# Splitting projected queries and keys into three bf16 parts: residuals by TensorE matmuls, or by VectorE subtractions in PSUM

## The reference, cut to what matters

```python
xn = _layernorm(x)
q, k, v = split(xn @ w_attn, 3)                 # 16 heads of 8 channels
scores = q @ k.T / sqrt(8) + causal + logw      # logw: a decay per head over the distance
att = softmax(scores); y = att @ v
out = x + y @ w_proj + moe(xn)                  # softmax router, top 2 of 8, silu, 128 -> 512 -> 128
```

## Time and profile before

| | |
|---|---|
| time, median of 3 runs | 726.49 us (723.21 to 731.6) |
| the profiled execution | 724.6 us, of which the span from first to last instruction is 722.8 us |
| PE busy | 580.9 us (80%) |
| POOL busy | 413.9 us (57%) |
| DVE busy | 340.2 us (47%) |
| ACT busy | 291.3 us (40%) |

### The profile page before, as it was taken

One profiled execution on the slowest core, in us unless ns is written; L12 is line 12 of the kernel. 1 busy time (PEld: TensorE's weight loads), 2 busy tenths in 40 slices (PEclk: granted clock), 3 DMA queues, 4 the chain that ended last, 5 costly groups with the idle time before them and its releaser, 6 DMA issues.

```text
span 722.8 us, 13966 instructions
## 1 busy us (share of the span) xinstructions
PE 580.9 (80%) x4558; PEld 396.4 (55%) x4572; DVE 340.2 (47%) x1396; ACT 291.3 (40%) x521; POOL 413.9 (57%) x674
## 2 busy tenths in 40 slices
PE   0696200999999999999999999999859998899840
PEld 0275000565555555565555555665558988898840
DVE  6504800466566565475565655677213222222225
ACT  7121000565555555555555555556512222222210
POOL 1300478777686677686786776789224444344432
PEclk9999999999999999999999999999969999999985
DMA  8952011222240331322312312310715565555538
GB/s 208 181 161 88 26 52 41 67 66 71 74 125 25 124 93 50 102 71 77 101 48 75 115 34 74 104 56 16 220 41 167 171 186 173 168 178 176 174 124 274
DMA packets 76564, 79.05 MB, mean 109 GB/s; under 512 B 8766, under 2 KB 59712, under 8 KB 76496
## 3 DMA queue, kind: packets, MB, share of 16 engines
q1 hardware_dynamic: 72144, 69.70, 34.4%
q0 software_dynamic: 4352, 8.47, 3.4%
HBM read 46.49 MB, written 30.02 MB: 106 GB/s over the span
## 4 chain that ended last, share of the span: by engine, by line
PE 71%; DVE 11%; POOL 5%; issue 5%; DMA 4%; SPq 2%; ACT 1%; POOLq 0%; DVEq 0%
PE psT L1014 18%; PE psO L1026 11%; PE ps L1104 11%; PE psT L1114 9%; PE psM L967 8%; PE ps L993 6%; DVE scores L881 5%; POOL rows_dram L592 4%; PE psO L957 2%; PE psM L976 1%; DMA x_all<-x 1%; PE psM L1095 1%; PE psM L969 1%; DVE x_all L428 1%; PE ps L1059 1%
## 5 line engine op out<-in xcount | busy, mean ns | idle before, releaser
L610 POOL TENSOR_SCALAR scores<-scores,row_max 128x256 f32<-128x256 f32 (+3 forms) x512 | 264.0, 533 | 92.0 <-DVE row_max L881 89.8
L881 DVE CUSTOM_DVE_ANT_0 scores<-ps,wdist 128x256 f32<-128x256 f32 (+3 forms) x512 | 222.2, 487 | 175.3 <-PE ps L993 175.2
L676 ACT ACTIVATE probs<-psT 128x512 f32<-128x512 f32 x320 | 173.9, 595 | 137.1 <-PE psT L1014 137.1
L1014 PE MATMUL psT<-ident,scores 128*128 128x128 f32 x1280 | 175.2, 281 | 36.5 <-POOL scores L610 36.5
L1014 PEld LDWEIGHTS psT<-ident,scores 128*128 128x128 f32 x1280 | 140.5, 142 | 74.3 <-POOL scores L610 47.7
L626 POOL DMA_INDIRECT picked_dram<-values,row_ring x72 | 70.7, 982 | 98.1 <-DVE values L924 93.0
L1026 PE MATMUL psO<-probs,values 128*32 128x512 f32 (+3 forms) x1024 | 94.8, 444 | 0.0
L712 ACT ACTIVATE probs<-ps 128x512 f32<-128x512 f32 x72 | 43.0, 597 | 126.6 <-PE ps L1104 126.6
L1104 PE MATMUL ps<-values,wdist 128*128 128x128 f32 x576 | 81.0, 285 | 12.4 <-issue 11.6
L1104 PEld LDWEIGHTS ps<-values,wdist 128*128 128x128 f32 x576 | 71.4, 196 | 18.9 <-issue 18.2
L1114 PE MATMUL psT<-wdist,probs 128*128 x576 | 77.3, 278 | 0.0
(11 more groups left out here) (119 smaller groups left out, 367.9 us busy)
## 6 DMA issues: line engine op xcount, KB each, us to landing
wdist<-w1t SPq DMA_DIRECT2D x72, 256.0 KB, 3.2
k_rows<-k_dram SPq DMA_DIRECT2D x64, 96.0 KB, 2.5
q_rows<-q_dram SPq DMA_DIRECT2D x64, 96.0 KB, 2.4
rows_dram<-probs SPq DMA_DIRECT2D x1, 4680.0 KB, 34.8
row_ring<-rows_dram SPq DMA_DIRECT2D x72, 65.0 KB, 2.5
probs<-picked_dram SPq DMA_DIRECT2D x8, 512.0 KB, 7.5
k_dram<-k_parts SPq DMA_DIRECT2D x8, 384.0 KB, 2.4
q_dram<-q_parts SPq DMA_DIRECT2D x8, 384.0 KB
```

The lines of the kernel that those rows point to most:

```text
L610: last = nc.gpsimd.tensor_scalar(part, part, -1.0, row_max[:, r, tile, quad:quad + 1], ALU.mult, ALU.add)
L676: nc.scalar.activation(probs[:, at.ring(2), w, :], psT[:, w % 2], ACT.Exp, scale=-1.0).then_inc(exp_ready, 1)
L881: last = nc.vector.tensor_tensor_reduce(out=scores[:, r, u, col:col + n], in0=bank[:, col:col + n], in1=wdist[:, at.g * QUADS + quad, SEQ ...
L1014: last = nc.tensor.transpose(psT[:, w % 2, place * P:(place + 1) * P], scores[:, at.ring(2), u, col + key * P:col + (key + 1) * P], ident[:])
```

## The change

The projection is made once per batch for keys and once for queries (KA, QA). Its hi part is rounded by ACT as before. The residual is no longer made anew by TensorE: DVE subtracts hi from `psM` in place (KR, QR, `rest_step`), ACT rounds what is left to mid (KM, QM, `mid_step`), and DVE subtracts mid from it and writes the result, rounded to bf16, as lo (KL, QL, `lo_step`). The steps KB, KC, QB, QC and the tile `minus_ident` go. `psM` stays taken from KA to KL. KR stands behind P1(1) in the slot, KM behind TE 2-4, KL behind TE 4-6 and PV 2 and ahead of P1(3). Three semaphores are new (`hi_ready`, `rest_ready`, `mid_ready`). In the start DVE runs the prologue's four subtractions after it has normalised batch 2.

```diff
+    per_batch("KR", -3)
+    per_batch("QR", -2)
     step("TE", n - 1, NGROUP, 2, 4)
     step("PV", n - 2, NGROUP, 1)
-    per_batch("KB", -3)
-    per_batch("QB", -2)
+    per_batch("KM", -3)
+    per_batch("QM", -2)
     per_batch("PJ", 8)
     step("P1", n, NGROUP, 2)
     step("TE", n - 1, NGROUP, 4, 6)
     step("PV", n - 2, NGROUP, 2)
+    per_batch("KL", -3)
+    per_batch("QL", -2)
     step("P1", n, NGROUP, 3)
     step("TE", n - 1, NGROUP, 6, 8)
     step("PV", n - 2, NGROUP, 3)
-    per_batch("KC", -3)
     per_batch("KW", -3)
-    per_batch("QC", -2)
     per_batch("QW", -2)
...
-PROLOGUE = [("KA", 0), ("KB", 0), ("KC", 0), ("KW", 0), ("QA", 0), ("QB", 0), ("QC", 0), ("QW", 0), ("V", 0),
+PROLOGUE = [("KA", 0), ("KR", 0), ("KM", 0), ("KL", 0), ("KW", 0), ("QA", 0), ("QR", 0), ("QM", 0), ("QL", 0), ("QW", 0),
+            ("V", 0),
             ("KD", 0), ("QD", 0)]
-MISC_KINDS = ("KA", "KB", "KC", "QA", "QB", "QC", "V", "NT", "YT", "PJ")
+MISC_KINDS = ("KA", "QA", "V", "NT", "YT", "PJ")
...
                 def keys_write(at):
-                    sp.wait_ge(misc_free, at.misc("KC", 1))
+                    sp.wait_ge(misc_free, at.misc("KA", 1))
...
+                def hi_step(kind, parts, written):
                     def step(at):
                         act.wait_ge(misc_full, at.misc(kind, 1))
-                        if number == 0 and at.c > 0:
+                        if at.c > 0:
                             act.wait_ge(written, at.batches(48))
-                        nc.scalar.activation(parts[:, number], psM[:], ACT.Copy).then_inc(misc_free, 1)
+                        nc.scalar.activation(parts[:, 0], psM[:], ACT.Copy).then_inc(hi_ready, 1)
+                def mid_step(number, parts):
+                    def step(at):
+                        act.wait_ge(rest_ready, at.batches(2, number))
+                        nc.scalar.activation(parts[:, 1], psM[:], ACT.Copy).then_inc(mid_ready, 1)
...
+                def rest_step(number, parts):
+                    def step(at):
+                        dve.wait_ge(hi_ready, at.batches(2, number))
+                        nc.vector.tensor_tensor(psM[:], psM[:], parts[:, 0], ALU.subtract).then_inc(rest_ready, 1)
+                def lo_step(number, parts):
+                    def step(at):
+                        dve.wait_ge(mid_ready, at.batches(2, number))
+                        nc.vector.tensor_tensor(parts[:, 2], psM[:], parts[:, 1], ALU.subtract).then_inc(misc_free, 1)
...
                 for b in range(1, BATCH):
                     normalise(b)
+                    if b == 2:
+                        run_prologue(number_parts)
...
                     def step(at):
                         misc_use(at, kind)
                         if kind == "KA" and (at.c >= 2 * GROUPS):
                             pe.wait_ge(xt_loaded, at.batches(16, -16))
-                        last = mm(psM[:], w, xt[:, at.parity, :], start=True, stop=not parts)
-                        for part in parts:
-                            last = mm(psM[:], minus_ident[:], part, start=False, stop=part is parts[-1])
-                        last.then_inc(misc_full, 1)
+                        mm(psM[:], w, xt[:, at.parity, :], start=True, stop=True).then_inc(misc_full, 1)
```

More of the change, by code:

```diff
@@ L121, in per_batch @@
             b = (n - phase) // GROUPS
-            if 0 <= b < BATCH and b >= {"XT": 2, "KA": 1, "KB": 1, "KC": 1, "KW": 1, "QA": 1, "QB": 1, "QC": 1, "QW": 1,
-                                          "V": 1}.get(kind, 0):
+            if 0 <= b < BATCH and b >= {"XT": 2, "V": 1}.get(kind, 0 if kind in ("YT", "PJ") else 1):
                 steps.append((kind, b * GROUPS - n))
@@ L259, in build @@
         ident = sb("ident", [P, P])
-        minus_ident = sb("minus_ident", [P, P], BF16)
         minus_half = sb("minus_half", [P, NTILE])
@@ L364, in build @@
         misc_free = sem("misc_free")
+        hi_ready = sem("hi_ready")
+        rest_ready = sem("rest_ready")
+        mid_ready = sem("mid_ready")
         k_written = sem("k_written")
@@ L654, in _ @@
                         last.then_inc(wdist_ready, 1)
-                def part_step(kind, parts, number, written):
+                def hi_step(kind, parts, written):
                     def step(at):
                         act.wait_ge(misc_full, at.misc(kind, 1))
-                        if number == 0 and at.c > 0:
+                        if at.c > 0:
                             act.wait_ge(written, at.batches(48))
-                        nc.scalar.activation(parts[:, number], psM[:], ACT.Copy).then_inc(misc_free, 1)
+                        nc.scalar.activation(parts[:, 0], psM[:], ACT.Copy).then_inc(hi_ready, 1)
+                    return step
+                def mid_step(number, parts):
+                    def step(at):
+                        act.wait_ge(rest_ready, at.batches(2, number))
+                        nc.scalar.activation(parts[:, 1], psM[:], ACT.Copy).then_inc(mid_ready, 1)
                     return step
@@ L766, in normalise @@
                     last.then_inc(xn_ready, 1)
+                def rest_step(number, parts):
+                    def step(at):
+                        dve.wait_ge(hi_ready, at.batches(2, number))
+                        nc.vector.tensor_tensor(psM[:], psM[:], parts[:, 0], ALU.subtract).then_inc(rest_ready, 1)
+                    return step
+                def lo_step(number, parts):
+                    def step(at):
+                        dve.wait_ge(mid_ready, at.batches(2, number))
+                        nc.vector.tensor_tensor(parts[:, 2], psM[:], parts[:, 1], ALU.subtract).then_inc(misc_free, 1)
+                    return step
+                number_parts = {"KR": rest_step(1, k_parts), "KL": lo_step(1, k_parts),
+                                "QR": rest_step(2, q_parts), "QL": lo_step(2, q_parts)}
                 dve.wait_ge(rstd_ready, 1)
@@ L959, in start_logits, with all_heads_step @@
                     return last
-                def all_heads_step(kind, w, parts):
+                def all_heads_step(kind, w):
                     def step(at):
@@ L1045, in pj_step @@
                     last.then_inc(misc_full, 1)
-                k_less, q_less = ([parts[:, 0], parts[:, 1]] for parts in (k_parts, q_parts))
-                w_k = w_qkv[:, C:2 * C]
-                parts = {"QA": all_heads_step("QA", w_q[:], []), "QB": all_heads_step("QB", w_q[:], q_less[:1]),
-                         "QC": all_heads_step("QC", w_q[:], q_less), "KA": all_heads_step("KA", w_k, []),
-                         "KB": all_heads_step("KB", w_k, k_less[:1]), "KC": all_heads_step("KC", w_k, k_less),
+                parts = {"QA": all_heads_step("QA", w_q[:]), "KA": all_heads_step("KA", w_qkv[:, C:2 * C]),
                          "V": v_step, "P1": p1_step, "TE": turn_step,
```

12 lines of the change are left out of this document (5 added, 7 removed).

## The result

The changed kernel takes 682.34 us (median of 4 executions, 674.33 to 683.83) against 726.19 us in the same comparison (median of 4, 723.21 to 731.6): 43.9 us less, ratio 0.9366 with a 95% interval of 0.9274 to 0.9457. Forecast were 679 us and 46.4 us less. The profiled execution took 682.88 us, its span 681.1.

The account below looks back on a forecast made before the run. PE was taken to bound the attention, with the prologue also on the path: 38.8 us from the slots plus 7.6 from the start, 46.4 in all, took the profiled 724.6 us to 678.2, forecast as a 679 us median, range 672 to 690.

Parts of the forecast that it names:

- PE is the bound: Attention: PE, busy 96% or more in K, Q and V slots, sets the pace; DVE and POOL keep up.
- 2.77 us a slot, 38.8 in all: Attention: dropping KB (1.28 us) and KC (1.49), likewise for queries, saves 2.77 us in each of 14 K and Q slots.
- The additions cost nothing at 0.69 us: K and Q slots: two added DVE subtractions of 0.69 us each fit without delaying PE.
- the two bounds: Price of one DVE subtraction: 0.4 us at the least, 1.4 us at the most, around the chosen 0.69.
- The margin: K and Q slots: DVE can run about 0.4 us late, ahead of P1(4), before PE is delayed.
- The late-DVE rival: K and Q slots: subtractions of 1.2 us or more, or a dearer crossing, make it 688 to 696 us; chance 0.10.
- The start, 7.6 us: Prologue: the shorter projection ladder brings the V step at 33.6 us instead of 41.28, moving all that follows.
- the clock rises later: Slot 1: fewer dense passes put off PE's clock rise; 690 us if by one slot, 682 if less; chance 0.06.
- the prediction's sign: Slot 1: the prediction is wrong if PE's doubled durations reach beyond 132 us minus the 7.6.
- That the start gives nothing: Prologue: DMA loads or DVE's hold-up replace the ladder, losing the 7.6 us, for 687 us; chance 0.08.
- The exposed handshake: K and Q slots: DVE, ACT, DVE lies open, PE idles 2 us and drops its clock, 783 us; chance 0.02.
- That another engine paces the attention: Attention: another engine holds slots at 13.97 us, so nothing measurable changes, 720 us or so; chance 0.01.

Follow-up runs that it names:

- the projection twice: Changed kernel with PE making the projection twice into the same bank in every K and Q slot of batches 1 to 7; 691.81 us.
- the slots alone: Changed kernel with only batches 1 to 7 split by subtractions, the prologue projecting three times as in the kernel before; 687.31 us, ratio 0.9602.
- the start alone: Changed kernel with only the prologue split by subtractions, batches 1 to 7 projecting three times as in the kernel before; 721.47 us, ratio 1.0031.
- the keys first: Changed kernel with DVE subtracting for the keys before normalising batch 1, and for the queries before normalising the rest; 676.68 us, ratio 0.9413.
- filled before: Kernel before the change, with a 128-column unread matmul behind each of its six prologue projections; 719.99 us, ratio 1.0044.
- the profile with the filled pauses: Changed kernel with the keys' subtraction ahead of normalising batch 1, plus one unread projection behind each of the prologue's two projections; 674.71 us, ratio 0.9392.

## Why the prediction was right

*PE is the bound.* Right. PE's work removed came out one to one, and the same 0.87 us put back in made the slot 0.87 longer (the projection twice), with DVE and POOL unchanged.

*2.77 us a slot, 38.8 in all.* Right. The K slot went from 13.97 to 11.20 or 11.21, as the check against the V slot said; 38.3 us were won between the first transposes and group 31, and 37 to 38 by the slots alone.

*The additions cost nothing at 0.69 us.* Right in price and result: 0.70 for PSUM into PSUM and 0.69 for PSUM into bf16, and PE's wait for `y` stayed at 0.35. The choice of L908's row over the two bounds was the right one, and the crossings into and out of KM did not show. The margin was mis-sized: 0.4 us forecast at one place, 0.51 measured at two (0.42 ahead of P1(4), 0.09 ahead of the reciprocal). DVE is 18 us busier and not 22, because the forecast counted each subtraction whole and they overlap with their neighbours. The late-DVE rival's condition, a subtraction of 1.2 us or more, never came; its price was too high as well: 1.21 us of added DVE work cost 0.53 a slot, where its rule of work less margin gives 0.7 to 0.8.

*The start, 7.6 us.* Right in mechanism, 1.2 us too much: V came 6.4 us earlier (34.89 against 41.28), and the first logits reduction too (56.21 against 62.59), so nothing was lost further on. By the prediction's own sign ("if the ladder of the start isn't shorter by 7 us") this part was wrong. The mis-sized term is "28 instructions take 8.54 us, so 8 take 2.44": they took 3.42, since four of those eight run beside GpSimd's selection. Another 0.4 is the later start of KA in this profile (22.59 against 22.16). Without it KR was at 26.26 and V at 33.21, and the forecast had 26.6 and 33.6.

*The clock of the start.* The rival "the clock rises later" had the price right in order of size and the place wrong. In slot 1 hardly anything was put off: the first transposes at full speed come 6.6 us behind the first in before (132.21) and 6.8 in the changed kernel (126.04). The last doubled ones end at about 125.8 and not by 124.4, as the prediction's sign wants; 1.2 of this is the start. The prologue is where it decides. The forecast took the durations of the one profile of before for the start of every execution; in 23 of 50 PE's clock rises there, and with the change it rose less often (4 of 26). Among executions that did not rise it is worth 727.9 - 682.5 = 45.4 us, near the 46.4; the medians as they come differ by 43.9, the two profiles by 41.7. So part of the nearness to 46.4 depends on which executions are compared. It is also why the start alone shows no gain in its ratio though its path is 6.7 us shorter: its unrisen executions (721.5) are 6.4 below those of before (727.9), but its risen one (718.6) is one in ten and before's (716.6) are half. What of this is shown: with PE's pauses filled the clock rose in all four kernels tried (30 of 30 executions), with either order. What is not shown: why the changed order alone rises less often, as the keys first rose in 4 of 6 with pauses of 2.8 us; where the 11.3 us between the two kinds of before lie, of which the one risen profile with the old start (the slots alone) has 5.6 ahead of the scores; and what makes the clock fall, which it did at 38 us under a PE busy throughout, with transposes and 8-column logits, while in filled before the same sequence ran at the upper level for 10 us (37.82 to 47.86). The Trainium skill, TensorE: Matmul & The Clock Gate, section Part 1, takes activity as what lifts the reduced clock; the filled pauses agree, the fall doesn't follow from any row here.

*The other rivals.* That the start gives nothing fell with V at 34.89 and the scores 6.4 us earlier; the 0.08 might have gone to the clock of the start. The exposed handshake that would make the kernel slower did not appear: PE is busy for 97% of K and Q slots, and its clock stays up. That another engine paces the attention was excluded by the slots as they came.

*The time.* 679 against 682.3: 1.2 us in the start, 0.5 in the slots, the rest, 1.6 us, lies within what the kinds of execution and the expert stage bring, the latter with 188.6 to 195.7 us over the profiles whatever the attention does.

## What to carry to other kernels

Price removed work by the same loop's iterations that already lack it: the V slot gave the new K slot's length to 0.04 us, and it said at the same time that no other engine would take over. Don't divide a group's time by its count where the instructions have different neighbours; list the ones that the change needs. Before trusting a stretch ahead of which PE has been idle, look at several executions' mean granted clock; the shorter ladder with longer pauses on PE had the upper level less often than the longer one, and unread matmuls in the pauses won some 5 us back in the changed kernel (676.9 against 682.0). In before they removed the slower kind, but the median stayed 3.4 us above the faster one.

## What the runs showed of the hardware

- The time of one and the same kernel has two kinds, 716.6 and 727.9 us (medians), told apart by the mean granted clock. In the profiles with 0.909 to 0.925 PE's clock rises in the start. While it is up, a batch of the start takes 1.28 us instead of 2.45.
- The clock falls back while PE is busy without a pause (5.97 of 6.00 us), about 6 us after the V step began, in the profile with the filled pauses; in filled before it stayed up for 10 us of the same transposes and logits. The granted column reads 1.00 until this first fall, whatever the level.
- Beside GpSimd's 128x512 selections DVE's 128x128 fp32 TENSOR_SCALAR takes about 0.6 us from start to start instead of 0.26, one of DVE's for each of GpSimd's; a subtraction with one input in PSUM takes 0.70 beside them and alone.
- A subtraction from PSUM into PSUM, in place, costs 0.70 us for 128x512, as much as one into SBUF (0.69); without a wait before it, it puts off what follows by 0.60.
- The last stretch, from the first expert matmul to the end, varied from 188.6 to 195.7 us over the profiles.
